# Four graph layers on one core: row turning, softmax sums, row lookups and the subtraction of the maximum rearranged in the edge passes

## The reference, cut to what matters

```python
edge_index = stack([src, dst])
x = ln(x + gnn0(x, edge_attr, edge_index))   # q*k*tanh(edge) logits, 16 heads, softmax by dst, MLP
x = ln(x + gnn1(x, edge_index))              # GAT with self loops, 4 heads, gelu
x = ln(x + gnn2(x, edge_index))              # two GATv2 layers with self loops (8 heads, 1 head), elu
x = ln(x + gnn3(x, edge_index, edge_attr))   # attention with edge term, 4 heads

# inside GATv2:
e = leaky_relu(xl[src] + xr[dst], 0.2);  logits = einsum('ehc,hc->eh', e, att)
ex = exp(logits - segment_max(logits, dst)[dst])
out = segment_sum(xl[src] * (ex / segment_sum(ex, dst)[dst])[..., None], dst)
```

## Time and profile before

| | us |
|---|---|
| runs, median of 3 | 4066.97 (4057.2 to 4076.98) |
| the profiled execution | 4061.93, its span 4060.2 |
| PE busy / DVE busy | 3500.2 (86%) / 3558.8 (88%) |
| ACT busy / POOL busy | 2879.2 (71%) / 2308.0 (57%) |
| edge passes 0, 1, 2a, 2b, 3 | 601.5, 562.2, 546.9, 529.1, 586.2 |

### The profile page before, as it was taken

The page is one execution under the profiler, slowest core; times in us unless marked ns, Lnnn a source line. Parts: engine busy times, 40 slices in busy tenths (PEclk is TensorE's granted clock), DMA queues, the critical chain, the costliest instruction groups (busy, mean ns, idle before and its releaser), DMA issues. The chain is left out here.

```text
span 4060.2 us, 72393 instructions
## 1 busy us (share of the span) xinstructions
PE 3500.2 (86%) x19961; PEld 2510.3 (62%) x20169; DVE 3558.8 (88%) x6756; ACT 2879.2 (71%) x9715; POOL 2308.0 (57%) x2305
## 2 busy tenths in 40 slices
PE   2999999999987999986999969999867777687775
PEld 2888888888864777764666645555534444354443
DVE  3899999999986999976999959999979999698786
ACT  2999999999975888875988855555546766344343
POOL 1577777777766777754433323345153442687777
PEclk9999999999988999998999989999989999898888
DMA  1455555555544343324544425555345554454442
GB/s 49 129 149 152 151 152 150 152 152 150 152 140 110 103 105 100 102 61 121 129 126 125 119 75 134 139 137 136 95 127 146 143 147 127 129 133 119 114 117 67
DMA packets 719120, 503.45 MB, mean 124 GB/s; under 512 B 141745, under 2 KB 621335, under 8 KB 718960
## 3 DMA queue, kind: packets, MB, share of 16 engines
q1 hardware_dynamic: 533072, 362.39, 33.0%
q0 software_dynamic: 56528, 81.64, 7.6%
q10 hardware_dynamic: 129360, 57.82, 5.1%
HBM read 304.28 MB, written 200.10 MB: 124 GB/s over the span
## 5 line engine op out<-in xcount | busy, mean ns | idle before, releaser
L1169 POOL DMA_INDIRECT slot_src_rows<-x,src_table_cols x392 | 420.7, 1073 | 453.1 <-PE psum L226 227.4
L237 ACT ACTIVATE node_z<-psum 128x128 f32<-128x128 f32 x1568 | 419.8, 325 | 22.5 <-PE psum L217 14.7
L1169 POOL DMA_INDIRECT slot2a_src_rows<-x,src_table_cols x196 | 220.5, 1125 | 335.0 <-PE psum L226 201.3
L646 ACT ACT_TABLE_LOAD x306 | 392.6, 1283 | 12.9 <-issue 7.7
L237 ACT ACTIVATION_READ_ACCUMULATOR node_z<-psum 128x1 f32 x1568 | 348.5, 227 | 0.0
L237 ACT ACTIVATE slot_logit<-psum 128x128 f32<-128x128 f32 x980 | 256.8, 279 | 125.9 <-PE psum L1337 99.8
L1169 POOL DMA_INDIRECT slot2b_src_rows<-xl,src_table_cols x196 | 198.2, 1011 | 257.1 <-PE psum L226 210.5
L1194 POOL DMA_INDIRECT out_nodes<-slot_new,out_index x196 | 243.0, 1240 | 59.8 <-issue 58.9
L1001 POOL DMA_INDIRECT node_gathered<-in_x,src_cols x196 | 235.8, 1203 | 47.0 <-issue 47.0
L1173 POOL DMA_INDIRECT slot_dst_rows<-in_x,dst_gather_cols x196 | 211.0, 1076 | 84.4 <-issue 50.9
L1166 POOL DMA_INDIRECT map_cols<-slot_map,src_cols x196 | 213.6, 1090 | 59.7 <-issue 59.7
(11 more groups left out here) (417 smaller groups left out, 12180.5 us busy)
## 6 DMA issues: line engine op xcount, KB each, us to landing
x<-node_x SPq DMA_DIRECT2D x294, 256.0 KB, 2.9
slot_neg<-neg SPq DMA_DIRECT2D x147, 256.0 KB, 4.5
node_xT<-in_x_T SPq DMA_DIRECT2D x98, 256.0 KB, 3.1
out_nodes<-node_x SPq DMA_DIRECT2D x98, 256.0 KB, 2.8
x<-slot_new ACTq DMA_DIRECT2D x98, 256.0 KB, 2.3
slot_keep<-keep SPq DMA_DIRECT2D x98, 256.0 KB, 4.2
slot_dst_rows<-x SPq DMA_DIRECT2D x98, 256.0 KB, 5.4
xl<-node_xl SPq DMA_DIRECT2D x98, 128.0 KB, 2.9
```

Of the source, the lines that this page charges most:

```text
L237: ins = act.activation(g.z[u][:, t, :], rows[:, t, :], ACT.Square, scale=float(D ** -0.5), accum_out=sums[u][:, t:t + 1])
L646: act.add_instruction(mybir.InstLoadActFuncSet(name=nc.get_next_instruction_name(), ins=[], outs=[], act_func_set_id=wanted[0]))
L1169: pool.indirect_dma_start(src_rows[u][:, t, 0:src_width], None, table, column(c.src_table_cols[order], u, i, t))\
```

## The change

- Pass 0 and pass 2a: `tot`, `rec`, `rs` and `rB` are gone. The denominators stand in all 128 partitions already; ScalarE takes their logarithm (`ln`) and the exponential of its negative (`inv`), and `agg` multiplies by that from SBUF. In 2a VectorE adds the self loop's part to the denominator first (`tot`, now a VectorE step).
- Pass 2a: `v` (source times `Wl1`) is made first and copied out by ScalarE; `Wr1` times destination is then accumulated onto the same bank, so that `z` has one product where it had two. The leaky relu is split in a relu on ScalarE and linear parts in `r`, which has four products of 512 columns in place of three and one of bf16. `o` takes bank B.
- Pass 2a and 2b: `z` on VectorE is gone; in 2b ScalarE makes a relu and a linear copy (`zl`), and `r` has two products. `e_p` moves from VectorE to TensorE: a product of minus the identity with the maximum is accumulated onto the logits. `exp` is split in `exp_p` (from PSUM) and `exp`, 512 columns each.
- Lookups: pass 0 looks up 116 of the 196 tiles, three for each chunk until they are done; pass 1 looks up the other 80, two for each chunk, and waits for them before it gathers by them. `source_columns` stands after pass 1.
- `srcT` of the next chunk in 2a waits for `exp_p` in place of `sv`.
- New `PLAN` lists for 0, 2a, 2b and 3; pass 1 keeps its list, with two more entries for each group. The chain of pass 3 is as before.

```diff
-        "2a": [("DVE", "dst"), ("PE", "z"), ("PE", "zo"), ("ACT", "z"), ("ACT", "zo"), ("DVE", "z"),
-               ("PE", "r"), ("PE", "v")],
-        "2b": [("DVE", "dst"), ("PE", "z"), ("ACT", "z"), ("DVE", "z"), ("PE", "r")],
+        "2a": [("PE", "v"), ("ACT", "v"), ("DVE", "dst"), ("PE", "z"), ("PE", "zo"), ("ACT", "z"), ("ACT", "zo"),
+               ("PE", "r"), ("PE", "o")],
+        "2b": [("DVE", "dst"), ("PE", "z"), ("ACT", "z"), ("ACT", "zl"), ("PE", "r")],
...
+    if layer in ("2a", "2b"):
+        softmax = [("DVE", "fc"), ("DVE", "f"), ("PE", "e_p"), ("DVE", "shift"), ("DVE", "e_c"), ("ACT", "exp_p"), ("ACT", "exp")]
     if layer == "0":
-        sums = [("DVE", "v"), ("DVE", "den"), ("DVE", "pv"), ("PE", "tot"), ("DVE", "num"), ("DVE", "tot")]
+        sums = [("DVE", "v"), ("DVE", "den"), ("DVE", "pv"), ("ACT", "ln"), ("DVE", "num"), ("ACT", "inv"), ("DVE", "agg")]
...
-        sums = [("ACT", "exps"), ("PE", "o"), ("DVE", "den"), ("DVE", "pv"), ("PE", "tot"), ("DVE", "num"), ("DVE", "sv"), ("DVE", "ns")]
+        sums = [("ACT", "exps"), ("DVE", "den"), ("DVE", "pv"), ("DVE", "num"), ("DVE", "sv"), ("DVE", "tot"), ("ACT", "ln"),
+                ("DVE", "ns"), ("ACT", "inv"), ("DVE", "agg")]
...
+    if layer in ("0", "2a"):
+        mean = []
...
     if layer == "0":
-        side += [("POOL", f"dst_gather{t}") for t in range(TILES)]
+        side = [("POOL", f"gather{t}") for t in range(3)] + [("POOL", f"dst_gather{t}") for t in range(TILES)]
+    elif layer == "1":
+        side += [("POOL", "gather_row0"), ("POOL", "gather_row1")]
```

```diff
+MAP_TURNS = 7
+MAP_FIRST = [tile for tile in range(SLOT_TILES) if tile // TILES < MAP_TURNS * STREAMS or tile // TILES == SLOT_CHUNKS - 1]
...
+def row_lookup(u, i, t):
+
+    turn = MAP_TURNS + (2 * i + t) // TILES
+    if turn * STREAMS + u < SLOT_CHUNKS - 1:
+        return (turn * STREAMS + u) * TILES + (2 * i + t) % TILES
+    return None
...
                     if t == 0:
                         pool.wait_ge(*g.PE.done(u, i, "srcT"))
+                        if lookups[u]:
+                            pool.wait_ge(looked_up[u], lookups[u] * 16)
                     gather_source(u, i + 1, t)
...
+                elif step == "ln":
+                    act.wait_ge(*g.DVE.done(u, i, "den"))
+                    act_copy(act, g, u, expo[u][:, 2, :], den[u][:, :], ACT.Ln, c.tiny[:, 0:1])
+                elif step == "inv":
+                    act.wait_ge(*g.ACT.done(u, i, "ln"))
+                    act_copy(act, g, u, expo[u][:, 2, :], expo[u][:, 2, :], ACT.Exp, scale=-1.0)
...
+                elif step == "z" and layer == "2a":
+                    pe.wait_ge(*g.ACT.done(u, i, "v"))
+                    pe.matmul(A(u), c.Wr1[:, :], dst, start=False, stop=True, skip_group_check=True).then_inc(g.pe_out[u], 1)
...
+                    pe.wait_ge(*g.ACT.done(u, i, "z"))
+                    pe.matmul(A(u), c.src_linear[:, :], src, start=True, stop=False)
+                    pe.matmul(A(u), c.own_linear[:, :], dst, start=False, stop=False)
+                    pe.matmul(A(u), c.src_relu[:, :], first, start=False, stop=False)
                     pe.wait_ge(*g.ACT.done(u, i, "zo"))
-                    pe.matmul(A(u), c.own_rows[:, 0:D], c.ones[:, :], start=True, stop=False)
-                    pe.matmul(A(u), c.own_linear[:, :], dst, start=False, stop=False)
-                    pe.matmul(A(u), c.own_relu[:, :], second, start=False, stop=False)
-                    pe.wait_ge(*g.DVE.done(u, i, "z"))
-                    pe.matmul(A(u), c.S1[:, :], first, start=False, stop=True).then_inc(g.pe_out[u], 1)
+                    pe.matmul(A(u), c.own_relu[:, :], second, start=False, stop=True).then_inc(g.pe_out[u], 1)
...
+                elif step == "e_p":
+
+                    pe.wait_ge(*g.DVE.done(u, i, "f"))
+                    pe.matmul((A if layer == "2a" else B)(u), c.minus_ident[:, :], fmax[u][:, 1:CHUNK + 1], start=False, stop=True,
+                              skip_group_check=True).then_inc(g.pe_out[u], 1)
...
-                    pe.wait_ge(*g.DVE.done(u, i, "z"))
-                    product(u, B, [(c.pair_gap[:, :], first)])
+                    pe.wait_ge(*g.ACT.done(u, i, "z"))
+                    pe.matmul(B(u), c.pair_relu[:, :], first, start=True, stop=False)
+                    pe.wait_ge(*g.ACT.done(u, i, "zl"))
+                    pe.matmul(B(u), c.pair_linear[:, :], second, start=False, stop=True).then_inc(g.pe_out[u], 1)
```

More of the change, by code:

```diff
@@ L626, in _ @@
                       start=True, stop=True).then_inc(turned, 1)
+            pe.wait_ge(source_float, 1)
+            pe.matmul(psum[:, 3, 0:SLOT_TILES], c.anti[:, :], src_float[:, :], start=True, stop=True).then_inc(source_back, 1)
             pe.wait_ge(firsts, 4)
@@ L1208, in _ @@
             if layer == "0":
-                pool.wait_ge(map_ready, SLOT_TILES * 16)
+                pool.wait_ge(map_ready, len(MAP_FIRST) * 16)
+            if layer == "1":
+                for u in g.streams:
+                    pool.wait_ge(looked_up[u], lookups[u] * 16)
             if layer == "3":
@@ L1250, in work @@
                     act_copy(act, g, u, t1[u][:, :], A(u), scale=SLOPE)
+                elif step == "exp_p":
+                    act.wait_ge(*g.PE.done(u, i, "e_p"))
+                    act_copy(act, g, u, expo[u][:, 0, :], (A if layer == "2a" else B)(u), ACT.Exp)
+                elif step == "exp" and layer in ("2a", "2b"):
+                    act.wait_ge(*g.DVE.done(u, i, "e_c"))
+                    act_copy(act, g, u, expo[u][:, 1, :], expo[u][:, 1, :], ACT.Exp)
                 elif step == "exp":
@@ L1256, in work @@
                     act_copy(act, g, u, expo[u][:, 2, :], fmax[u][:, 1:CHUNK + 1], ACT.Exp, scale=-1.0)
+                elif step == "ln" and layer == "2a":
+                    act.wait_ge(*g.DVE.done(u, i, "tot"))
+                    act_copy(act, g, u, expo[u][:, 2, :], expo[u][:, 2, :], ACT.Ln)
+                elif step == "ln":
[4 more added lines that the diff above has]
+                    act_copy(act, g, u, expo[u][:, 2, :], expo[u][:, 2, :], ACT.Exp, scale=-1.0)
                 elif step == "rs":
@@ L1348, in work @@
                     elif layer == "2a":
-                        pe.wait_ge(*g.DVE.done(u, i - 1, "sv"))
+                        pe.wait_ge(*g.ACT.done(u, i - 1, "exp_p"))
                     elif layer in ("0", "1"):
@@ L1390, in work @@
                     product(u, B, [(c.self_gap[:, :], logit[u])])
+                elif step == "v" and layer == "2a":
+                    pe.wait_ge(*g.DVE.done(u, i, "dst"))
+                    pe.matmul(A(u), c.Wl1[:, :], src, start=True, stop=True).then_inc(g.pe_out[u], 1)
                 elif step == "z" and layer == "2a":
-                    pe.wait_ge(*g.ACT.done(u, i, "srcT"))
-                    pe.wait_ge(*g.DVE.done(u, i, "dst"))
-                    product(u, A, [(c.Wl1[:, :], src), (c.Wr1[:, :], dst)])
+                    pe.wait_ge(*g.ACT.done(u, i, "v"))
+                    pe.matmul(A(u), c.Wr1[:, :], dst, start=False, stop=True, skip_group_check=True).then_inc(g.pe_out[u], 1)
                 elif step == "zo":
@@ L1638, in work @@
                     ins = v.tensor_tensor(small[u][:, :, :], sums(u), small[u][:, :, :], ALU.add)
+                elif step == "tot" and layer == "2a":
+                    after("den")
+                    after("sv")
+                    ins = v.tensor_tensor(expo[u][:, 2, :], den[u][:, :], expo[u][:, 2, :], ALU.add)
                 elif step == "tot":
@@ L1641, in work @@
                     ins = v.tensor_scalar(small[u][:, :, :], sums(u), SOFTMAX_EPS, None, ALU.add)
-                elif step == "rec" and layer in ("2a", "2b"):
+                elif step == "rec" and layer == "2b":
                     v.wait_ge(*g.PE.done(u, i, "tot"))
@@ L1647, in work @@
                     ins = v.reciprocal(recip[u][:, :, :], small[u][:, :, :])
+                elif step == "agg" and layer in ("0", "2a"):
+                    after("ns" if own else "num")
+                    v.wait_ge(*g.ACT.done(u, i, "inv"))
+                    ins = v.tensor_tensor(agg[u][:, :], (t2 if own else num)[u][:, :], expo[u][:, 2, :], ALU.mult)
                 elif step == "agg":
```

130 lines of the change are left out of this document (74 added, 56 removed), and 38 rows, old and new, of the table PLAN.

## The result

The changed kernel took 3929.76 us (median of 4 runs, 3928.13 to 3930.92) against 4067.98 for the kernel before in the same session: ratio 0.966, 95% interval 0.964 to 0.9681. The profiled execution took 3930.92 us with a span of 3929.2, 131.0 less than before. The windows of the changed kernel come first: five whole edge passes, then a steady stretch of passes 0, 2a, 2b and 3, in the columns of the earlier trace rows.

The account below looks back on a forecast made before the run. TensorE and GpSimd were taken to fill pass 0, TensorE and VectorE 2a, VectorE 2b, GpSimd pass 3. Gains 34 + 30 + 42 = 106 us off 4061.9 gave 3956, predicted as 3960 us; range 3912 to 4020.

Parts of the forecast that it names:

- I am wrong if pass 3's length moves by more than 10 us: Pass 3: one of the prediction's own signs of error; it forecast gain 0, at most 8 us either way.
- its pitches for 2a and pass 3: Forecast distance between chunks' `f` scans: 9.6 to 9.9 us in 2a, about 11.1 in pass 3.
- PE is last at 10.52, with ACT right behind: Pass 0: TensorE sets the pitch at 10.52 us, ScalarE near; 10.70 with stalls, gain 34 us.
- The drain of some 1.38 us for each table switch: Pass 0: the skill's rule, not adopted, putting ScalarE at 11.3 us and the gain at 4 us.
- relief of one alone is worth only that: Pass 0: TensorE and GpSimd are limits within 0.4 us of each other, so relieving one gains only that.
- Two engines at 9.6 do not interlock perfectly; I take 9.78: Pass 2a: pitch 9.78 us over TensorE's 9.63 and VectorE's 9.55; gain 30 us, between 0 and 37.
- `e_p`'s cover: Pass 2a: 3.2 us of other TensorE work between `r` and `e_p` covers the 1.24 us scan `f`.
- The ring: Pass 2b: TensorE steps, scan `dst`, then `z`, `y2`, `r` make 8.9 us; 9.05 taken, gain 42 us.
- its 586 us are 392 x 1.49. A better order on the others can't shorten that: Pass 3: GpSimd's 392 DMAs fix its length, so the new order gains 0, at most 8 us either way.
- TensorE never stood at `e_p`: Rival 3, 2a and 2b: TensorE waits 2.5 us per chunk for scan `f` at `e_p`; 4170 us, chance 0.06.
- lost in a ring: Rival 1, whole kernel: half of each gain goes in waits between engines; 4009 us, chance 0.21.
- The forecast of reached floors: Rival 2, whole kernel: passes 0, 2a, 2b gain 42 + 37 + 57 = 136 us; 3920 us, chance 0.11.

Follow-up runs that it names:

- experiment 1: The changed kernel with only pass 3's order list put back to the old one: 3969.57 us, ratio 0.9754 to the kernel before.
- experiment 10: The kernel before with three shared-row lookups a chunk in pass 0 and 49 left for the end of GpSimd's queue: 4089.44 us, ratio 1.006.
- experiment 9: The changed kernel with all 196 shared-row lookups back in pass 0, four a chunk, none in pass 1: 3935.65 us, ratio 0.9683.
- experiment 8: The changed kernel with ScalarE issuing pass 2a's two row stores behind its copy `v` instead of in front: 3909.55 us, ratio 0.962.
- Experiment 11: The changed kernel with 2b's subtraction of the running maximum back on VectorE: 3966.44 us, ratio 0.9753.
- experiment 2: The kernel before with only pass 3's order list replaced by the new one: 4032.91 us, ratio 0.9922.
- experiment 3: Six stages added behind the changed kernel, 24 GpSimd lookups each, alone or beside one VectorE instruction kind: 947 ns alone, 1878 beside scans with two SBUF operands.
- experiment 6: The changed kernel with pass 3 in the old order and only its `f` scan reading PSUM: 3925.67 us, ratio 0.9649.

## Why the prediction was right and where it was wrong

The forecast was 3960 us, and 3929.76 lies in its range. Taken by passes from the profiled execution, the forecast was 3956 and the measurement 3931. Pass 3 gave 40 us that the sum did not have, 2a gave 17 and 2b 7 less than it had, and pass 0 and the rest 9 more. That the total lies in the range says nothing for pass 3: experiment 1, without pass 3's gain, reads 3969.57, in the range as well. By its own sign ("I am wrong if pass 3's length moves by more than 10 us") the prediction was wrong there, and its pitches for 2a and pass 3 were missed.

- **Pass 0: right.** Pitch 10.67 against 10.70, pass -38.7 against -34. TensorE is 453 of 460 us busy and ScalarE 418, so the step "PE is last at 10.52, with ACT right behind" fits. No run takes the turning of rows back by itself, so this rests on the sum and on these shares. The logarithm of 512 columns, which I took at 0.62 between 0.30 and 1.24, has a mean of 712 ns in the trace after. The drain of some 1.38 us for each table switch, by the Trainium skill ("ScalarE: Activation LUTs", What ACT_TABLE_LOAD costs), would have left a pitch of 11.3; neither the pitch of 10.67 nor the records show it: at the 305 switches of the trace after, the next activation starts 1.30 us after the load does, in the median, and the load 0.02 after the instruction before it. Of "relief of one alone is worth only that", experiment 10 confirms one half: without TensorE's relief GpSimd's gives nothing. The other half was wrong in size. Eight DMAs at 1.374 us would have held the pitch at 10.99 and left 0.4 us of gain; in experiment 9 GpSimd is full with eight at a pitch of 10.76, 1.345 each, so TensorE's relief alone gives 0.64 of the 0.73.
- **Pass 2a: the term was mis-sized.** "Two engines at 9.6 do not interlock perfectly; I take 9.78": the pitch was 10.11. The allowance over the floor was 0.15 and should have been 0.48. The floor of 9.63 that I summed from the earlier trace rows is what experiment 8 measured (9.64), with both engines full, so the reason that I gave for the allowance was wrong too: two engines at 9.6 did interlock. What I left out is the queue ahead of a wait that the change adds: `z` waits for ScalarE's `v`, and in front of `v` stand `xlr` and two store issues that no busy time shows. I had checked `e_p`'s cover and not this one. With the stores gone from the ring TensorE is full, at the sum of its start-to-start distances, while weight loads are busy 54% of the time. The Trainium skill ("Perfetto Trace Analysis", Identifying the Most-Contended Engine) has the busy share of weight loads as one of its two measures of TensorE's headroom; it would have misled here.
- **Pass 2b: right.** The ring gave 8.9 and I took 9.05; measured 9.14, -34.8 us against -42. Experiment 11 shows that the subtraction on TensorE carries it. Whether the ring or VectorE's own work sets the 9.14 is not told apart by any run: VectorE is busy 392 of 400 us there and TensorE 388.
- **Pass 1 and what lies ahead of pass 0: right,** -1.8 and -2.7 us, the second just outside the 2 us that I allowed. The two lookups more in pass 1 cost nothing that can be seen.
- **Pass 3: wrong,** and the step is "its 586 us are 392 x 1.49. A better order on the others can't shorten that". The first half stands: GpSimd fills the pass in both kernels. The second took 1.49 us for a property of the DMA. It was 0.30 of issue and an average of 1.18 over DMAs that last 0.95 alone and up to 1.93, a few 2.02, when they start inside a VectorE scan of two SBUF operands. The order decides how many do: experiments 1 and 2 show it for the pass, the count of 104 against 60 for the meetings, experiments 3 and 6 for the operand. The earlier trace rows had it in view: means of 1256 and 1132 ns, where experiment 3 has 947 for a lookup alone. I read the mean and not the spread.
- **The rivals.** TensorE never stood at `e_p` for long: in 2a it idled 1.3 us in 440 there. More than half of the gain was lost in a ring in 2a, a sixth in 2b, none elsewhere. The forecast of reached floors, 3920, is near the time by accident: it had nothing for pass 3 and too much for 2a.

## What to carry to other kernels

When one engine fills a stage, look at the spread of its instructions and not the mean alone, and set each long one against what the other engines ran at its start; here a queue of equal DMAs lost some 80 us of 578 (390 x (1179 - 970) ns), some 72 of them to the scans and 8 to the products of another engine. Look at the spread in a probe as well: a mean can hide that nearly all the starts fell where one instruction follows another. Where a change adds a wait, write down everything ahead of the releasing instruction in its engine's queue, store issues too. A cure that lets an instruction read elsewhere may hold that place longer: price the new wait before the old one is gone.
